# The Hadamard turn of W2 without its trip through DRAM, weight units in more staging places, and the weight sums' transfers interleaved by group

## The chip, the cores and the metric

The program runs on one core of a Trainium2 chip. The metric is the device time of one execution in microseconds. The core has five engines with an instruction queue each: PE (TensorE: matmuls, with PEld for its weight loads), DVE (VectorE), ACT (ScalarE), POOL (GpSimd) and SP (SyncE, which here only issues transfers). SP's transfers stand in the hardware queue of the DMA engines, POOL's in the software queue.

## The reference

The input x is 16 sequences of 256 tokens and 512 channels, in float32.

```python
def fwht(x):                       # along the last axis (2048), times 1/sqrt(2048)
    ...
def _L0_ffn_ref(x, W1, W2, W3):
    up_gate = jnp.einsum('bsd,hd->bsh', x, W1)
    up_lin = jnp.einsum('bsd,hd->bsh', x, W3)
    hidden = jax.nn.silu(up_gate) * up_lin
    hidden = fwht(hidden)
    out = jnp.einsum('bsh,dh->bsd', hidden, W2)
    return out
x = x + jnp.tanh(g_xattn[0]) * _L0_xattn_ref(16, 256, 512, L0_xattn_time_decay, L0_xattn_time_first, _layernorm(x, axis=-1), ctx_2048)
x = x + jnp.tanh(g_ffn[0]) * _L0_ffn_ref(_layernorm(x, axis=-1), L0_ffn_W1, L0_ffn_W2, L0_ffn_W3)
```

`_L0_xattn_ref` is a scan over the 256 tokens of a sequence with an exponential decay for each channel (numerator and denominator). The hidden width is 2048. The transform of `hidden` is moved into W2: the kernel transforms W2 once and never the hidden values.

## The kernel before

The 4096 tokens go in 8 chunks of 512 tokens, two sequences each. A `Run` is what is done for one chunk; the first chunk is split into `Run(0)` and `Run(1)` (sequence a and b), and the others are runs 2 to 8. Every engine has its own list of instructions, written out by hand, with semaphore waits between the lists.

**Weights in three-pass form.** Every float32 weight is split into a float16 part and a bfloat16 rest (`hi` and `lo`), and each product is three matmuls. W1 and W3 come in 16 units of 128x1024 (`units`, 0.5 MB each; two units make a piece of W1 and W3 of 256 hidden channels). SP's `load_unit(n)` brings a unit to one of six staging places (`raw`), ACT's `unit_hi(n)` writes the float16 part to `wts`, DVE's `unit_lo(n)` clamps it and writes the rest, and `raw_lo` counts that. `put_plain(p)` then stores piece p in `up_stage` in DRAM.

**W2.** Its four quarters (`load_rows(q)`, 1 MB each) lie in the upper half of `wts`. PE's `mix_rows(i)` multiplies one of 16 tiles with the 128x128 Hadamard matrix `had`, ACT's `keep_rows(i)` copies it to `mixed`, SP's `put_rows(q)` stores a quarter in DRAM and `turn_rows(q)` reads it back turned. PE's `mix_slots(i)` multiplies with `across` (the 16x16 part of the transform), ACT's `tile_hi`, POOL's `tile_clamp`, PE's `less_hi` and ACT's `tile_lo` split the tile into the two parts of `w2`.

**The first chunk.** PE's `ahead(a, j)` does hidden tiles 0 to 3 of sequence a; `ffn(b)` then does, in 16 slots j, the gate and the linear product of tile j (both sequences from j = 4) and the down product of tile j - 2. On DVE each slot has `hidden_tile` and `hidden_lo`, and between them the scan and norm of run 2 (`FIRST_AT` says in which slot), units (`unit_slot`) and weight sums (`SUMS_AT`). DVE works through this list in order: what waits in it holds all behind it.

**The weight sums.** Runs 2 to 8 use a scheme with 7 products of blocks in place of 8, for which sums of blocks of W1 and W3 are needed. POOL makes them in DRAM, for four groups of four units: `copy_group(g)` copies, `add_first(g)` adds 1 MB, `add_rest(g)` adds twice 0.5 MB, each behind the landing of the one before. SP's `load_again(n)` loads the summed unit n (to one of three places `traw`), DVE's `weight_parts(n)` splits it, and SP's `put_sums(n)` stores it to `up_stage` from one of two places `tout`, which must have been stored before it is written again.

**Runs 2 to 8.** `pairs` walks over 8 pairs of hidden tiles; SP's `load_pair` brings 2 MB of `up_stage` for each to a ring of two places. `load_pair(Run(2), 0)` and `(Run(2), 1)` are the first two, and `put_factors` and `spread_factors` send the layer norm's factors through DRAM.

## Time and profile before

| | |
|---|---|
| median of 3 runs | 1058.53 us (1057.27 to 1059.4) |
| the profiled execution | 1057.33 us, span 1055.5 us |
| PE busy | 1000.7 us (95%) |
| DVE busy | 801.5 us (76%) |
| first pair of run 2 begins on PE | 214.71 us |
| DMA | 218.40 MB, mean 207 GB/s |

The span is from the first to the last instruction, and times in the trace are counted from its start. A busy share is an average over stages with different limits: the first 215 us are the first chunk and all preparation of weights, and the rest is runs 2 to 8. The share of a DMA queue is the time of its packets as a share of the time of 16 DMA engines.

### The profile page before, as it was taken

How to read it: one execution, taken by the hardware profiler on the slowest of the kernel's cores; microseconds unless marked ns; L12 is line 12 of the kernel's file. 1: busy time of each engine (PE TensorE's matmuls, PEld its weight loads, DVE VectorE, ACT ScalarE, POOL GpSimd, SP SyncE). 2: the span in 40 equal slices, each digit the busy share in tenths (PEclk: the TensorE clock that was granted, in tenths of full speed). 3: DMA queues.
4: the chain of work that ended last, by engine and by line, in shares of the span. 5: the costliest groups of instructions: out<-in, count | busy, mean ns of one | idle time of the engine just before them, and what ended most of it. 6: DMA issues, size and time to landing. Idle time of an engine off the chain costs nothing.

```text
span 1055.5 us, 17259 instructions
## 1 busy us (share of the span) xinstructions
PE 1000.7 (95%) x6826; PEld 685.7 (65%) x6892; DVE 801.5 (76%) x1304; ACT 440.8 (42%) x736; POOL 252.4 (24%) x196
## 2 busy tenths in 40 slices
PE   5789689989999999999999999999999999999998
PEld 2355334456677777767776777767777677767775
DVE  7966598899989994889668994899669994753333
ACT  6756351346243542444243542445243532522221
POOL 0142121111432124221322124222322124111111
PEclk9898899999999999999999999999999999999999
DMA  9999999995885446454645446454645433444331
GB/s 355 347 396 266 312 255 292 245 322 192 302 289 182 153 167 240 114 221 148 257 161 180 155 165 240 115 222 147 256 160 180 173 116 151 161 170 157 125 149 41
DMA packets 49729, 218.40 MB, mean 207 GB/s; under 512 B 9456, under 2 KB 26992, under 8 KB 38512
## 3 DMA queue, kind: packets, MB, share of 16 engines
q1 hardware_dynamic: 40816, 200.52, 52.8%
q0 software_dynamic: 8832, 16.78, 7.7%
q8 instruction: 54, 0.88, 0.3%
q14 instruction: 27, 0.22, 0.1%
HBM read 187.90 MB, written 46.16 MB: 222 GB/s over the span
## 4 chain that ended last, share of the span: by engine, by line
PE 66%; DVE 13%; DMA 11%; issue 5%; ACT 3%; SPq 1%; POOL 0%; another core or an unknown queue 0%; DVEq 0%; ACTq 0%
PE pl L730 8%; PE pl L732 8%; PE pl L731 8%; PE po L742 7%; PE po L744 7%; PE pg L730 6%; PE pg L732 6%; PE pg L731 6%; PE po L753 4%; PE po L751 3%; DMA up_sums<-w_t 2%; DVE work L1600 2%; DMA factor_rows<-tiny 2%; DVE x L1427 2%; DMA up_stage<-wts 2%
## 5 line engine op out<-in xcount | busy, mean ns | idle before, releaser
L1745 POOL TENSOR_TENSOR work<-work 128x512 bf16<-128x512 f32 x112 | 163.7, 1462 | 594.5 <-DVE work L1600 594.5
L742 PE MATMUL po<-work,w 128*128 128x512 f16 x456 | 173.0, 379 | 2.1 <-DVE x L1427 1.2
L744 PE MATMUL po<-work,w 128*128 128x512 f16 x456 | 172.8, 379 | 0.0
L1062 ACT ACTIVATE work<-work 128x256 f32<-128x256 f32 x168 | 68.4, 415 | 210.4 <-DVE work L1507 210.3
L730 PE MATMUL pg<-wts 128*128 128x256 f16 x448 | 122.5, 273 | 3.9 <-DVE work L1507 3.8
L1507 DVE TENSOR_TENSOR work<-pl,wts 128x256 f32<-128x256 f32 x168 | 65.1, 414 | 80.3 <-PE pl L732 77.7
L730 PE MATMUL pl<-wts 128*128 128x256 f16 x448 | 122.1, 273 | 0.6 <-ACT wts L1036 0.6
L731 PE MATMUL pg<-wts 128*128 128x256 bf16 x448 | 122.4, 273 | 0.0
L732 PE MATMUL pg<-wts 128*128 128x256 f16 x448 | 122.4, 273 | 0.0
L730 PE MATMUL pl<-xn,wts 128*128 128x256 f16 x448 | 122.3, 273 | 0.0
L731 PE MATMUL pl<-xn,wts 128*128 128x256 bf16 x448 | 122.3, 273 | 0.0
L732 PE MATMUL pl<-xn,wts 128*128 128x256 f16 x448 | 122.2, 273 | 0.0
L732 PE MATMUL pl<-wts 128*128 128x256 f16 x448 | 122.1, 273 | 0.0
L731 PE MATMUL pl<-wts 128*128 128x256 bf16 x448 | 122.1, 273 | 0.0
L1600 DVE TENSOR_SCALAR work<-work 128x512 f16<-128x512 f32 x112 | 90.4, 808 | 7.9
L753 PE MATMUL po<-work,w 128*128 128x512 bf16 x228 | 86.4, 379 | 2.9
L1036 ACT COPY wts<-pg 128x512 f32<-128x512 f32 x56 | 32.6, 582 | 122.8 <-PE pg L732 122.8
L742 PEld LDWEIGHTS po<-work,w 128*128 128x128 f16 x456 | 44.6, 98 | 52.3 <-DVE x L1427 9.3
L744 PEld LDWEIGHTS po<-work,w 128*128 128x128 bf16 x456 | 44.6, 98 | 39.6
L730 PE MATMUL pg<-xn,wts 128*128 128x256 f16 x224 | 61.3, 274 | 6.3 <-DVE work L1383 3.6
L1507 DVE TENSOR_TENSOR work<-pg,early 128x256 f32<-128x256 f32 x56 | 23.6, 421 | 55.7 <-PE pg L732 54.8
L751 PE MATMUL po<-work,w 128*128 128x512 bf16 x172 | 65.2, 379 | 0.0
(201 smaller groups left out, 2132.8 us busy)
## 6 DMA issues: line engine op xcount, KB each, us to landing
wts<-up_stage SPq DMA_DIRECT2D x56, 2048.0 KB, 7.9
up_stage<-wts SPq DMA_DIRECT2D x8, 1024.0 KB, 11.8
up_stage<-wts SPq DMA_DIRECT2D x16, 512.0 KB, 8.4
ev<-ctx_t SPq DMA_DIRECT2D x7, 1024.0 KB, 11.3
xin<-x_t SPq DMA_DIRECT2D x7, 1024.0 KB, 8.2
bv<-x_tok SPq DMA_DIRECT2D x7, 1024.0 KB, 10.5
out_t<-x SPq DMA_DIRECT2D x7, 1024.0 KB, 4.8
wts<-up_sums SPq DMA_DIRECT2D x11, 512.0 KB, 11.4
```

The source lines that it names most:

```text
L730: pe.matmul(bank, hi, ah, start=(start and k == 0), stop=False, skip_group_check=True)
L731: pe.matmul(bank, hi, al, start=False, stop=False, skip_group_check=True)
L732: mm = pe.matmul(bank, lo, ah, start=False, stop=(stop and k == 1), skip_group_check=True)
L742: pe.matmul(po[:, d, :], w2h[:, j, d * P:d * P + P], hh[:, b, :], start=start, stop=False, skip_group_check=True)
L744: pe.matmul(po[:, d, :], w2l[:, j, d * P:d * P + P], hh[:, b, :], start=False, stop=False, skip_group_check=True)
L751: pe.matmul(po[:, d, :], w2h[:, j + 1, d * P:d * P + P], hl[:, b + 1, :], start=False, stop=False, skip_group_check=True)
L753: pe.matmul(po[:, d, :], w2h[:, j, d * P:d * P + P], hl[:, b, :], start=False, stop=((p - 1) % PAIRS == PAIRS - 1), skip_group_check=True) ...
L1036: act.copy(early1[:, w, :], chain_fifth[w]).then_inc(kept1, 1)
L1062: act.activation(sg[:, slot, cols], src, ACT.Silu, scale=(1.0, -1.0)[slot]).then_inc(acted, 1)
L1507: dve.tensor_tensor((sg, hf)[w][:, slot, b * T:b * T + T], bank, other, ALU.add).then_inc(joined, 1)
L1600: dve.tensor_scalar(hh[:, 2 * (p % 2) + slot, :], hf[:, slot, :], F16_MAX, -F16_MAX, ALU.min, ALU.max).then_inc(pair_hi, 1)
L1745: pool.tensor_tensor(hl[:, b, :], hf[:, slot, :], hh[:, b, :], ALU.subtract).then_inc(pair_lo, 1)
```

## The change

**W2.** The order of the two multiplications is swapped: W2 comes in another order of rows and columns, `mix_slots(i)` is now four float32 matmuls with the weight block as stationary operand and `across` as moving operand (128 columns each), which also turns the block; ACT's `keep(i)` copies the bank, with its columns permuted, to `mixed`, and `mix_rows(i)` multiplies with `had` from there. `put_rows`, `turn_rows` and the DRAM buffer `turn` are gone. **Units.** `raw` has 14 places, eight of them in the rows of W2 that have been used (`places`), so units 2 to 15 have waits on `slots_mm` and `rows_mm`. **Slots.** Units 14 and 15 are split in slot 12 of `ffn(b)`, and weight sum 3 moves from slot 8 to slot 5. **Sums.** POOL issues `copy_group(0)` behind the third clamp, and its `ffn` sends the first adds of group g + 1 and the copy of group g + 2 ahead of the third add of group g. **Orders.** The lists of SP, PE, ACT and DVE are written out anew, so that `over(a)` and `residual(a, 0)` stand ahead of the scans of sequence b.

```diff
 BETWEEN = {0: (), 1: (), 2: (10,), 3: (11,), 4: (13,), 5: (15,)}
@@ -71,7 +70,7 @@
...
-        raw = [psum2[:, :, :].rearrange("p k n -> p (k n)"), wide[:, 0:2, :].rearrange("p k n -> p (k n)"),
-               half1[:, 0:unit], half1[:, unit:], xn1[:, 0:unit], xn1[:, unit:]]
+        raw = ([psum2[:, :, :].rearrange("p k n -> p (k n)"), wide[:, 0:2, :].rearrange("p k n -> p (k n)")]
+               + [r[:, h * unit:(h + 1) * unit] for r in rows for h in range(2)]
+               + [r[:, h * unit:(h + 1) * unit] for r in (half1, xn1) for h in range(2)])
...
+        unit_slot = {0: (8, 9), 1: (10, 11), 3: (12,), 4: (13,), 12: (14, 15)}
+        places = (0, 1, 2, 3, 4, 5, 0, 1, 6, 7, 8, 9, 10, 11, 12, 13)
+
+        def uses(n):
+
+            return places[:n + 1].count(places[n])
...
+                if uses(n) > 1:
+                    sp.wait_ge(raw_lo, n - 5)
+                elif 2 <= places[n] < 10:
+                    sp.wait_ge(slots_mm, KT * (places[n] // 2))
+                elif places[n] >= 10:
+                    sp.wait_ge(rows_mm, KT * (places[n] // 2 - 2))
                 w, p = units[n]
-                sp.dma_start(raw[place_of[n]], raw_in[w][p]).then_inc(raw_loaded[place_of[n]], 16)
+                sp.dma_start(raw[places[n]], raw_in[w][p]).then_inc(raw_loaded[places[n]], 16)
 
             def load_rows(q):
                 sp.dma_start(rows[q], w2_in[q]).then_inc(rows_loaded[q], 16)
-
-            def put_rows(q):
-                sp.wait_ge(kept, KT * q + KT)
-                sp.dma_start(turn[q], mixed[q].rearrange("p (j d) -> p j d", d=P)).then_inc(put[q], 16)
-
-            def turn_rows(q):
-                sp.wait_ge(put[q], 16)
-                sp.dma_start(rows[q].rearrange("p (s d) -> p s d", d=P),
-                             turn[q].rearrange("(s r) j d -> (r j) s d", r=PS)).then_inc(turned[q], 16)
...
-            put_rows(0)
             load_half_x(1)
-            put_rows(1)
-            turn_rows(0)
-            put_rows(2)
-            turn_rows(1)
-            put_rows(3)
-            turn_rows(2)
-            for n in range(2, 4):
-                load_unit(n)
-            turn_rows(3)
-            for n in range(4, 6):
-                load_unit(n)
-            load_v(1)
-            for n in range(6, 10):
+            for n in range(2, 8):
                 load_unit(n)
             put_plain(0)
+            load_v(1)
+            load_unit(8)
+            load_unit(9)
             put_plain(1)
+            load_unit(10)
+            load_unit(11)
             load_x(1)
+            load_unit(12)
+            load_unit(13)
             sp.wait_ge(xn_turned, 4)
             load_tokens(1)
-            load_unit(10)
-            load_unit(11)
             put_plain(2)
-            load_unit(12)
-            load_unit(13)
+            load_unit(14)
+            load_unit(15)
+            put_plain(3)
             for n in range(0, 3):
                 load_again(n)
-            put_plain(3)
-            load_unit(14)
-            load_unit(15)
             put_plain(4)
...
             put_sums(1)
             put_plain(6)
+            load_again(4)
             put_sums(2)
-            put_plain(7)
+            load_again(5)
+            put_sums(3)
+            load_again(6)
             load_v(2)
-            load_again(4)
-            load_again(5)
+            put_sums(4)
+            load_again(7)
             load_x(2)
             load_tokens(2)
-            put_sums(3)
-            load_again(6)
-            put_sums(4)
-            load_again(7)
             put_sums(5)
+            put_plain(7)
+            put_factors(Run(3))
             load_pair(Run(2), 0)
-            put_factors(Run(3))
             put_sums(6)
             spread_factors(Run(3))
...
+            def mix_slots(i):
+
+                pe.wait_ge(rows_loaded[i // KT], 16)
+                wait(pe, kept, i)
+                for g in range(BLOCKS):
+                    col = (i % KT * BLOCKS + g) * P
+                    mm = pe.matmul(po[:, 2, g * P:(g + 1) * P], rows[i // KT][:, col:col + P], across,
+                                   start=True, stop=True)
+                mm.then_inc(slots_mm, 1)
+
             def mix_rows(i):
-                pe.wait_ge(rows_loaded[i // KT], 16)
-                wait(pe, kept, i - KT + 1)
-                pe.matmul(po[:, i % KT, :], had, tile_rows(i), start=True, stop=True).then_inc(had_mm, 1)
-
-            def mix_slots(i):
-                pe.wait_ge(turned[i // KT], 16)
-                if i < W2_BANKS:
-                    pe.wait_ge(kept, TILES)
-                wait(pe, w2_lo, i - W2_BANKS + 1)
-                pe.matmul(po[:, i % W2_BANKS, :], across, tile_rows(i), start=True, stop=False,
-                          skip_group_check=True).then_inc(blk_mm, 1)
+
+                pe.wait_ge(kept, i // KT * KT + KT)
+                wait(pe, w2_lo, i - 2)
+                pe.matmul(tile_banks[i % 3], had, mixed[i // KT][:, (i % KT) * TOK:(i % KT + 1) * TOK],
+                          start=True, stop=False, skip_group_check=True).then_inc(rows_mm, 1)
...
             scan(a, v, bv, scan_a)
             with_token(a, v, bv, scan_a, num_done)
             weigh(b)
+            over(a)
+            residual(a, 0)
             scan(b, ea, eb, scan_b)
-            over(a)
+            unit_lo(0)
+            x1_moments_of(0)
+            scan(b, v, bv, scan_a)
+            with_token(b, v, bv, scan_a, num_done)
+            unit_lo(1)
             with_token(b, ea, eb, scan_b, den_done)
-            residual(a, 0)
-            scan(b, v, bv, scan_a)
-            x1_moments_of(0)
-            for n in range(0, 2):
+            turned_lo(0)
+            for n in range(2, 4):
                 unit_lo(n)
-            turned_lo(0)
-            with_token(b, v, bv, scan_a, num_done)
             over(b)
             residual(b, 1)
-            dve.wait_ge(put[0], 16)
-            dve.wait_ge(put[1], 16)
-            hidden_tile(a, 0)
-            for n in range(2, 4):
-                unit_lo(n)
+            dve.wait_ge(rows_mm, 2 * KT)
+            for j in range(0, 2):
+                hidden_tile(a, j)
+            unit_lo(4)
             x1_moments_of(1)
-            for j in range(1, 3):
+            unit_lo(5)
+            for j in range(2, 4):
                 hidden_tile(a, j)
             turned_lo(1)
-            hidden_tile(a, 3)
-            unit_lo(4)
+            for n in range(6, 8):
+                unit_lo(n)
...
-                    tile_clamp(i)
-                add_rest(0)
-                for g in range(1, len(GROUPS)):
-                    copy_group(g)
-                    add_first(g)
-                    add_rest(g)
+                for g in range(len(GROUPS)):
+                    add_second(g)
+                    if g + 1 < len(GROUPS):
+                        add_first(g + 1)
+                    if g + 2 < len(GROUPS):
+                        copy_group(g + 2)
+                    add_third(g)
...
-            hidden_lo(Run(0), 0)
-            for i in range(6, 8):
+            copy_group(0)
+            for i in range(3, 11):
                 tile_clamp(i)
-            hidden_lo(Run(0), 1)
-            copy_group(0)
-            for i in range(8, 11):
+            pool.wait_ge(rows_mm, 2 * KT)
+            for j in range(0, 2):
+                hidden_lo(Run(0), j)
+            add_first(0)
+            copy_group(1)
+            for i in range(11, 13):
                 tile_clamp(i)
             for j in range(2, 4):
                 hidden_lo(Run(0), j)
-            add_first(0)
+            for i in range(13, TILES):
+                tile_clamp(i)
             ffn()
```

The list of POOL, which issues all transfers of the weight sums. Before, from the first clamps of W2 (L1682) on; L1677 is the low part of a hidden tile, L1694 a copy of a group, L1705 the first adds, L1714 the second and L1717 the third:

```order
L1682 TENSOR_SCALAR w<-w 128x4x128 x2
L1677 TENSOR_TENSOR work<-work 128x256
L1694 DMA up_sums<-w_t 16x16384 x2
L1682 TENSOR_SCALAR w<-w 128x4x128 x3
L1677 TENSOR_TENSOR work<-work 128x256 x2
L1705 DMA up_sums<-w_t 512x1x256 x2
L1682 TENSOR_SCALAR w<-w 128x4x128 x5
L1714 DMA up_sums<-up_sums 256x256 x2
L1717 DMA up_sums<-up_sums 256x256 x2
L1694 DMA up_sums<-w_t 16x16384 x2
L1705 DMA up_sums<-w_t 512x1x256 x2
```

And now, from the first copy on (L1695 clamps, L1690 low parts, L1707 copies, L1718, L1727 and L1734 first, second and third adds):

```order
L1707 DMA up_sums<-w_t 16x16384 x2
L1695 TENSOR_SCALAR w<-w 128x4x128 x8
L1690 TENSOR_TENSOR work<-work 128x256 x2
L1718 DMA up_sums<-w_t 512x1x256 x2
L1707 DMA up_sums<-w_t 16x16384 x2
L1695 TENSOR_SCALAR w<-w 128x4x128 x2
L1690 TENSOR_TENSOR work<-work 128x256 x2
L1695 TENSOR_SCALAR w<-w 128x4x128 x3
L1727 DMA up_sums<-up_sums 256x256 x2
L1718 DMA up_sums<-w_t 512x1x256 x2
L1707 DMA up_sums<-w_t 16x16384 x2
L1734 DMA up_sums<-up_sums 256x256 x2
```

The third adds of group 0, on which the first `load_again` waits, have moved behind the copy of group 1, the first adds of group 1 and the copy of group 2.

The list of SP at the same place. Before, from the tokens of run 2 (L409) on; L377 loads units, L418 is `put_plain`, L429 `load_again`, L435 `put_sums`:

```order
L409 DMA bv<-x_tok 128x2x1024
L377 DMA xn<-w_t 128x1024 x2
L418 DMA up_stage<-wts 128x4096
L377 DMA psum<-w_t 128x1024
L377 DMA wide<-w_t 128x1024
L429 DMA wts<-up_sums 128x1024 x2
L429 DMA spare<-up_sums 128x1024
L418 DMA up_stage<-wts 128x4096
L377 DMA xn<-w_t 128x1024 x2
L418 DMA up_stage<-wts 128x4096 x2
L435 DMA up_stage<-wts 128x2048
L429 DMA wts<-up_sums 128x1024
```

And now, from units 8 and 9 on (L379 loads units, L399 x, L402 the tokens, L411 is `put_plain`, L422 `load_again`, L428 `put_sums`):

```order
L379 DMA wts<-w_t 128x1024 x2
L411 DMA up_stage<-wts 128x4096
L379 DMA wts<-w_t 128x1024 x2
L399 DMA xin<-x_t 128x2048
L379 DMA x<-w_t 128x1024 x2
L402 DMA bv<-x_tok 128x2x1024
L411 DMA up_stage<-wts 128x4096
L379 DMA xn<-w_t 128x1024 x2
L411 DMA up_stage<-wts 128x4096
L422 DMA wts<-up_sums 128x1024 x2
L422 DMA spare<-up_sums 128x1024
L411 DMA up_stage<-wts 128x4096 x2
```

All units and `put_plain(3)` now stand ahead of the first `load_again`; before, two units and `put_plain(3)` stood behind it, ahead of the first `put_sums`.

## Rows read from the trace of the kernel before

**Rows 1.** The page: DMA busy tenths in 40 slices; shares of the last chain.

```profile
DMA  9999999995885446454645446454645433444331
...
PE 66%; DVE 13%; DMA 11%; issue 5%; ACT 3%; SPq 1%; POOL 0%; another core or an unknown queue 0%; DVEq 0%; ACTq 0%
```

**Rows 2.** Stages by window: PE, PEld, DVE, ACT, POOL busy, clock, DMA share, GB/s.

```profile
0.00:59.00 59.00, 40.08 (x132) 20.65 (x133) 48.51 (x99) 39.93 (x64) 7.76 (x15) 0.88 0.99 354
...
112.00:133.00 21.00, 12.88 (x51) 5.75 (x50) 15.18 (x21) 6.63 (x7) 1.03 (x2) 0.76 1.09 342
...
150.00:215.00 65.00, 58.53 (x257) 26.07 (x260) 55.07 (x81) 22.39 (x25) 13.11 (x13) 0.97 0.98 236
```

**Rows 3.** The chain that ended last, 60 to 150: start, us, what.

```profile
65.37 9.23 DMA up_sums<-w_t
...
74.90 15.42 DMA up_sums<-w_t
...
90.61 4.12 DMA up_sums<-up_sums
...
95.01 4.74 DMA up_sums<-up_sums
...
99.83 11.37 DMA wts<-up_sums
...
113.20 17.14 DMA up_stage<-wts
```

**Rows 4.** Timeline of PE: start, us, what, in brackets the idle time before and its releaser.

```profile
124.43 1.09 PE L589 MATMUL pst<-mats,bv 128*128 128x128 f32 x4 [8.07 <-ACT ev L881]
...
214.71 0.37 PE L730 MATMUL pg<-xn,wts 128*128 128x256 f16 x1 [3.64 <-DVE work L1383]
...
232.30 0.28 PE L730 MATMUL pg<-xn,wts 128*128 128x256 f16 x1 [1.36 <-DMA wts<-up_stage]
```

**Rows 5.** Timeline of DVE, the same columns.

```profile
111.22 0.69 DVE L1446 TENSOR_SCALAR wts<-wts 128x1024 f16<-128x1024 f32 x1 [5.30 <-DMA wts<-up_sums]
...
115.02 0.42 DVE L1433 TENSOR_SCALAR wts<-wts 128x1024 f16<-128x1024 f16 x1
...
116.62 0.42 DVE L1433 TENSOR_SCALAR wts<-wts 128x1024 f16<-128x1024 f16 x1
...
130.44 0.69 DVE L1446 TENSOR_SCALAR wts<-spare 128x1024 f16<-128x1024 f32 x1 [5.16 <-DMA up_stage<-wts]
...
176.59 2.35 DVE L1322 TENSOR_TENSOR eb<-x,pst 128x1024 f32<-128x1024 f32 x2 [3.76 <-PE pst L620]
...
200.83 0.69 DVE L1446 TENSOR_SCALAR wts<-wts 128x1024 f16<-128x1024 f32 x1 [2.86 <-DMA up_stage<-wts]
```

**Rows 6.** DMA queues: whole span, 0 to 59, 98 to 133, 104 to 107.

```profile
q0 software_dynamic: 8832, 16.78, 7.7%
...
q1 hardware_dynamic: 7903, 20.86, 98.7%
...
q1 hardware_dynamic: 1597, 7.48, 57.4%
q0 software_dynamic: 1642, 3.65, 45.8%
...
q0 software_dynamic: 32, 1.05, 93.3%
```

**Rows 7.** Timelines of ACT and POOL around the first hidden tiles.

```profile
53.43 0.38 ACT L961 ACTIVATE work<-pg 128x256 f32<-128x256 f32 x1
...
56.53 0.39 ACT L961 ACTIVATE work<-pg 128x256 f32<-128x256 f32 x1 [1.26 <-PE pg L656]
...
54.84 0.71 POOL L1677 TENSOR_TENSOR work<-work 128x256 bf16<-128x256 f32 x1 [1.36 <-DVE work L1390]
```

**Rows 8.** Timeline of PE: float32 matmuls of W2 and float32 transposes of x1.

```profile
13.12 4.46 PE L630 MATMUL po<-wts,mats 128*128 128x512 f32 x10
...
33.69 0.66 PE L603 MATMUL pst<-mats,x 128*128 128x128 f32 x4 [1.32 <-DVE x L1305]
34.19 0.60 PE L603 MATMUL pg<-mats,x 128*128 128x128 f32 x4
```

More of the change, by code:

```diff
@@ L707, in ffn @@
                     if j == 0:
-                        for i in range(11, 14):
-                            mix_slots(i)
-                        less_hi(11)
-                    if j == 1:
-                        less_hi(12)
-                        mix_slots(14)
-                        mix_slots(15)
                         for i in range(13, TILES):
@@ L1121, in _ @@
+            tile_hi(0)
             unit_hi(0)
-            for i in range(9, 16):
-                keep_rows(i)
-            unit_hi(1)
+            keep(5)
+            tile_lo(0)
+            for i in range(1, 3):
+                tile_hi(i)
+            keep(6)
+            unit_hi(1)
+            tile_lo(1)
+            unit_hi(2)
+            keep(7)
+            unit_hi(3)
+            tile_lo(2)
+            keep(8)
+            for i in range(3, 5):
+                tile_hi(i)
+            keep(9)
@@ L1125, in _ @@
+            tile_lo(3)
+            x1_normalise(0)
+            keep(10)
+            for i in range(5, 7):
+                tile_hi(i)
+            turned_hi(0)
+            tile_lo(4)
+            keep(11)
+            for i in range(5, 7):
+                tile_lo(i)
+            tile_hi(7)
             logs(b)
+            keep(12)
             inverses(b)
-            for i in range(0, 2):
-                tile_hi(i)
-            x1_normalise(0)
-            tile_hi(2)
-            for i in range(0, 2):
-                tile_lo(i)
@@ L1133, in _ @@
[L1133 to L1149 removed]
+            tile_lo(7)
@@ L1150, in _ @@
+            keep(13)
+            act.wait_ge(rows_mm, KT)
+            silu(a, 0)
             for i in range(8, 11):
                 tile_hi(i)
-            turned_hi(1)
+            silu(a, 1)
             unit_hi(4)
-            silu(a, 3)
+            keep(14)
+            unit_hi(5)
+            keep(15)
             for i in range(8, 11):
                 tile_lo(i)
+            x1_normalise(1)
+            silu(a, 2)
+            for i in range(11, 13):
+                tile_hi(i)
+            silu(a, 3)
@@ L1157, in _ @@
+            tile_lo(11)
+            turned_hi(1)
+            tile_lo(12)
+            for i in range(13, 16):
+                tile_hi(i)
+            for n in range(6, 8):
+                unit_hi(n)
             ffn(b)
@@ L1714, in add_rest, with add_third @@
                     pool.dma_start(sums[w][:, 3 * half:], sums[w][:, 0:half], accum_op=ALU.add).then_inc(summed[g][w], 16)
+            def add_third(g):
+                sums, half = group(g)[1], unit // 4
                 for w in range(2):
@@ L1807 @@
         had = np.block([[had, had], [had, -had]])
-    across = np.kron(np.eye(PS, dtype=np.float32), had[0:SLOTS, 0:SLOTS]) / np.float32(32)
+    across = np.kron(had[0:SLOTS, 0:SLOTS], np.eye(PS, dtype=np.float32)) / np.float32(32)
     gates = np.broadcast_to(np.concatenate([np.asarray(g_xattn), np.asarray(g_ffn)]), (P, 2))
```

174 lines of the change are left out of this document (77 added, 97 removed).

## The prediction

> **What bounds the kernel now.** I read the page first. The last chain is two thirds PE, and the DMA engines are at nine tenths for the first ninth of the span and at four to six tenths behind it [rows 1]. The change touches nothing behind the first pairs of run 2, so I looked at the time until that run's first pair begins on PE, 214.71 us [rows 4]. By stages [rows 2] PE has 12.88 of 21 us in 112 to 133 and 58.53 of 65 us in 150 to 215, DVE 15.18 and 55.07, while the DMA share stays at about 1.0 from the start to 215. So neither engine is full, and the DMA engines are.
>
> The waits say who is late. PE's longest is 8.07 us, ended at 124.43; before the first pair it waits 3.64 us for DVE's hidden tile 15, and before the second 1.36 us for the ring's load [rows 4]. DVE waits 5.30 us for the first loaded weight sum (until 111.22), 5.16 us for a place of `tout` to be stored (130.44), 3.76 us for the channel mean, on PE, and 2.86 us for `tout` again [rows 5]. The chain shows where the first comes from: copy of group 0 at 65.37, first adds at 74.90, second at 90.61, third at 95.01, `load_again(0)` from 99.83 to its landing 11.37 us later, and then `put_sums(0)`, 17.14 us [rows 3]. Behind slot 3 of `ffn(b)` DVE's list therefore runs from the landing of the first sum (call it T, 111.22) to PE's first pair at 214.71: 103.5 us, of which 5.16 + 3.76 + 2.86 = 11.8 us are waits. So what decides is when T falls, and what waits are left behind it.
>
> **The change part by part.**
>
> *The turn removed.* 4 MB are no longer written and 4 MB no longer read, 8.4 MB of the hardware queue. In 0 to 59 that queue moved 20.86 MB in 98.7% of 59 us, 2.8 us per MB [rows 6]: 23.4 us of the DMA engines are freed before 59. That is worth time only if something waits for the engines there; the next step asks that.
>
> *PE's work for W2.* Sixteen products with `across` become 64 of 128 columns with a weight load each. The trace has no such float32 matmul. Before, five of 512 columns (x10 in the row: two passes each) take 4.46 us [rows 8], 0.86 us with overlap taken off; a transpose with its own float32 load has a pitch of (34.19 - 33.69)/4 = 0.125 us [rows 8], so four matmuls of two passes lie between 0.86 us (by columns, loads hidden) and 1.0 us (eight such pitches). At half clock both double. I take 0.9, equal to what it replaces: nothing, 2 us over all 16 at most, hidden behind DVE's scans. The Trainium skill (TensorE: Matmul & The Clock Gate, Weight-path perf modes) says that fast weight loads are not to be had for float32. By the row they are hidden all the same; if they were not, each load being as long as its matmul, 14 us of PE work would be added ahead of slot 0.
>
> *ACT's, DVE's and POOL's lists until the first adds.* `add_first(0)` now stands behind the low parts of hidden tiles 0 and 1 of sequence a. Before, `silu` of these ended at 53.8 and 56.9, and a low part ended 2.1 us behind its `silu`'s start [rows 7]. ACT's list up to the first of them loses two copies of W2 and gains seven splits of about 0.5 us, 2.5 us, and loses waits for `load_unit` and `less_hi` that were about as long; DVE's has one product of 1.7 us more ahead of the first up tile, which then begins near 47. I take the two `silu` at 53.5 and 55.8, the low part at 58, and the first adds, which take a moment to issue, as work from 59.6 on (74.90 before [rows 3]).
>
> *The queue of POOL from there.* The sums cost 7.7% of 1055.5 = 81.3 us of all 16 engines for four groups, 20.3 each. A copy of 1.05 MB takes 93.3% of 3 us = 2.8 [rows 6], so a group's two take 5.6 and its adds 14.7 us: first 7.35, second 3.7, third 3.7. Ahead of the third add of the group's first half stand now: first adds of groups 0 and 1 (14.7), copies of 1 and 2 (11.2), second adds of 0 (3.7), and half a third (1.85): 31.4 us. Before it was half of that, with the copy. In the same time SP sends units 10 to 15, x, tokens, and `put_plain` 2 and 3: 7 MB, 7.34 in the row's unit, at 57.4% of 35 us for 7.48 MB, 2.7 us per MB [rows 6], 19.8 us. Both queues share the engines: in 98 to 133 the sum is 103% [rows 6]. (31.4 + 19.8)/1.03 = 49.7, so the sum is complete at 59.6 + 49.7 = 109.3. Then the load: 11.37 us before, when two copies were in the way [rows 3], and at least the 4.12 us of the shortest transfer of sums there; now small packets of adds are in the way, and I take 5.7. **T = 115.0**, against 111.22. The freed 23.4 us lie ahead of 59, where the queues now run dry, and the interleaving spends the 15 us by which the first adds start earlier.
>
> This T doesn't hang on DVE: before, it was ready at 111.22 - 5.30 = 105.9 [rows 5], and units 2 to 11 come sooner now, so it is ready between 97 and 106.
>
> *Behind T.* One unit fewer is split there (three for four): 116.62 - 115.02 = 1.6 us [rows 5]. `put_sums(0)` finds two `put_plain` ahead of it where three and two units stood, so its wait falls from 5.16 to about 4; sum 3 is now in slot 5 too and must wait for `put_sums(1)`, 2.5 (from 0 to 6: a store of 0.5 MB at full rate up to the 17.14 us of row 3); the mean's 3.76 goes, since DVE arrives later than PE there; the 2.86 goes, since sums 6 and 7 now stand in two slots, but ACT's root is then waited for, 0.8. Waits: 11.8 becomes 7.3. T to first pair: 103.5 - 1.6 - 4.5 = 97.4, and the pair begins at 212.4, 2.3 us earlier.
>
> *Ring and factors.* `put_factors` now stands ahead of the 2 MB load. Its wait for the factors held SP, and with that pair 1's load, so that PE waited 1.36 us [rows 4]; this goes. `put_plain(7)` now stands ahead of the first ring load and waits for unit 15, split in slot 12 some 18 us before the pair; the load of 2 MB needs 5.7 us of the engines, which are by then rid of the sums.
>
> The sum: 2.3 + 1.4 = 3.7 us. From the profiled execution's 1057.33 us that is 1053.6, and its time is 1.2 us under the median of the runs. From the median it is 1054.8. **I predict 1054 us.**
>
> **The rivals.** About 0.2%, 2.1 us, is what a measurement of this kernel can tell from no change.
>
> *The first sum is in time.* If the adds were as cheap per byte as loads, or overlapped with them, T would be set by DVE. With T between 97 and 106 and 94 to 97 us behind it, the pair begins at 191 to 203: 13 to 25 us faster, 1033 to 1046. For it speaks that DVE and PE are both short of full [rows 2]; against it the adds' 1 KB packets, 81 us for 16.78 MB [rows 6]. The Trainium skill's fit (DMA: Bandwidth & Descriptors, Anatomy of one DMA) gives the moving part of a transfer as its bytes at 436 GB/s, which for the 31.4 us would be about 15 and T would be DVE's. The trace disagrees: 81.3 us against 38.
>
> *Slower.* One mechanism: copies of later groups stand in the engines when SP's loads and stores of sums come, as at 99.83, where a load took 11.37 and the store 17.14 us [rows 3]. The load then costs 5.7 more, and the waits for both places of `tout` about 5.6 more: 3.7 faster becomes 7.6 slower, 1062 to 1066. It decides from T = 118.7 on, 3.7 us past mine.
>
> *No difference.* The part ahead of T gives exactly what it takes and only the ring's 1.4 us are left; or the turn wasn't on any path. 1057 to 1060.
>
> **How the numbers follow.** Chances: my forecast (1048 to 1056) 0.40, first sum in time 0.18, no difference 0.20, slower 0.22. Of the forecast's cases some 0.03 lie within 2.1 us of before. So faster 0.55, same 0.23, slower 0.22. The forecast's own range is 1048 to 1056; for 8 in 10 I go down into the first rival's middle, 1040, and up to 1064.
>
> **What would show it.** Right: first adds near 58 (POOL), the DMA share under a half between 37 and 58, the third add of group 0 landing at 107 to 113, DVE idle 10 us or more ahead of its first weight sum at about 115, then short waits for stores in slot 5, and the first pair at 212 with PE waiting for DVE's hidden tile 15. Wrong: a first sum before 105, which makes it much faster; ACT so late in the first 60 us that the first adds start past 65; or a wait of DVE for `tout` over 8 us in slot 5.

## The result, and the profile after

The changed kernel takes 1068.1 us (median of 6 runs, 1067.02 to 1068.79), the kernel before 1058.46 us beside it (6 runs, 1056.18 to 1059.4). The ratio is 1.0093, 95% interval 1.0075 to 1.0112: slower, where the prediction said 1054 us, and above the range's end of 1064.

The profiled execution has a span of 1066.9 us, 11.4 more than before. The page of the changed kernel, its DMA slices and the shares of its last chain, which answer to [rows 1]:

```profile
DMA  9599998586585546355554456254745434444331
...
PE 68%; DVE 16%; DMA 8%; issue 5%; ACT 3%; DVEq 0%; SPq 0%; POOL 0%; ACTq 0%
```

The page only tells that the engines of the DMA are now less full in the second slice (26.7 to 53.3). The place is told by the windows (columns as in [rows 2]; the last line is the kernel before):

```profile
0.00:59.00 59.00, 40.85 (x230) 30.60 (x230) 50.05 (x102) 43.20 (x70) 13.48 (x22) 1.00 0.80 297
...
37.00:58.00 21.00, 16.44 (x105) 11.22 (x104) 20.20 (x37) 17.31 (x28) 4.30 (x6) 1.00 0.75 279
...
133.00:150.00 17.00, 5.80 (x27) 2.45 (x25) 9.41 (x9) 0.00 (x0) 4.06 (x4) 0.78 1.04 271
...
133.00:150.00 17.00, 16.95 (x79) 7.74 (x79) 15.79 (x13) 7.52 (x10) 3.51 (x5) 1.00 1.08 325
```

The DMA share until 59 fell from 0.99 to 0.80: the freed time is there. But in 133 to 150 PE works 5.80 of 17 us (16.95 before) and ACT not at all, while the DMA engines are full. The chain of the changed kernel, which answers to [rows 3], says what they carry:

```profile
76.17 14.14 DMA up_sums<-up_sums
...
90.60 20.51 DMA up_sums<-up_sums
111.20 8.90 DMA wts<-up_sums
120.13 0.70 DVE wts L1457
125.52 0.70 DVE wts L1457
127.50 14.85 DMA up_stage<-wts
142.44 0.70 DVE wts L1457
```

The second adds of group 0 go out at 76.17 (90.61 before), but the third adds, issued at 90.60, take 20.51 us where they took 4.74. The first load starts at 111.20 and T, DVE's first work on a loaded sum, is 120.13, against 111.22. Then a place of `tout` waits 14.85 us for its store. The timelines of DVE, PE and ACT of the changed kernel, in the columns of [rows 4, 5]:

```profile
120.13 0.69 DVE L1457 TENSOR_SCALAR wts<-wts 128x1024 f16<-128x1024 f32 x1 [22.21 <-DMA wts<-up_sums]
138.28 0.69 DVE L1457 TENSOR_SCALAR wts<-spare 128x1024 f16<-128x1024 f32 x1 [8.88 <-DMA up_stage<-wts]
142.44 0.69 DVE L1457 TENSOR_SCALAR wts<-wts 128x1024 f16<-128x1024 f32 x1 [2.20 <-DMA up_stage<-wts]
187.03 2.35 DVE L1333 TENSOR_TENSOR eb<-x,pst 128x1024 f32<-128x1024 f32 x2 [2.52 <-PE pst L603]
223.57 0.68 DVE L1394 TENSOR_TENSOR work<-work,pl 128x512 f32<-128x512 f32 x1
...
154.51 0.59 PE L641 MATMUL pg<-xn,wts 128*128 128x512 f16 x1 [15.71 <-ACT work L960]
226.06 0.39 PE L710 MATMUL pg<-xn,wts 128*128 128x256 f16 x1 [3.80 <-DMA wts<-up_stage]
...
151.32 2.56 ACT L895 ACTIVATE ev<-ev,cc 128x512 f32<-128x512 f32 x4 [26.67 <-DVE eb L1263]
```

PE's 15.71 us are put down to ACT, but ACT stood still until 151.32: it waited for DVE's scan of run 2 (L1263), and the scan stands in DVE's list behind the two waits for `tout`. The first pair of run 2 begins at 226.06, 11.35 us later than before, and behind it both kernels need 840.8 us (1055.5 - 214.71 and 1066.9 - 226.06). So the loss lies ahead of the first pair: 8.9 us until T, 1.7 us of the ring's load (PE starts 1.81 us behind the end of DVE's hidden tile 15 at 224.25, and 0.15 us before), and 0.8 us between.

### The profile page after: what moved, and what is told of

Same layout as the page of the kernel before. It is cut to its first block, busy times and chain, and to the rows that moved or that the text cites. A ratio compares the mean times of both kernels' runs of the same rounds, so it can differ in the third digit from the quotient of the medians.

```text
span 1066.9 us, 17504 instructions
## 1 busy us (share of the span) xinstructions
PE 1003.7 (94%) x6988; PEld 694.6 (65%) x6988; DVE 802.4 (75%) x1304; ACT 440.0 (41%) x736; POOL 254.1 (24%) x196
## 4 chain that ended last, share of the span: by engine, by line
PE 68%; DVE 16%; DMA 8%; issue 5%; ACT 3%; DVEq 0%; SPq 0%; POOL 0%; ACTq 0%
PE pl L712 8%; PE pl L710 8%; PE pl L711 8%; PE po L722 7%; PE po L724 7%; PE pg L710 6%; PE pg L712 6%; PE pg L711 6%; PE po L733 4%; PE po L731 4%; DMA up_sums<-up_sums 3%; DVE x L1438 2%; DMA wts<-up_stage 2%; DVE work L1611 2%; DMA up_stage<-wts 1%
## 5 line engine op out<-in xcount | busy, mean ns | idle before, releaser
L731 PE MATMUL po<-work,w 128*128 128x512 bf16 x228 | 86.4, 379 | 0.0
L733 PE MATMUL po<-work,w 128*128 128x512 bf16 x228 | 86.4, 379 | 0.0
L724 PEld LDWEIGHTS po<-work,w 128*128 128x128 bf16 x456 | 44.6, 98 | 39.3
```

The source lines that it names most:

```text
L724: pe.matmul(po[:, d, :], w2l[:, j, d * P:d * P + P], hh[:, b, :], start=False, stop=False, skip_group_check=True)
L731: pe.matmul(po[:, d, :], w2h[:, j + 1, d * P:d * P + P], hl[:, b + 1, :], start=False, stop=False, skip_group_check=True)
L733: pe.matmul(po[:, d, :], w2h[:, j, d * P:d * P + P], hl[:, b, :], start=False, stop=((p - 1) % PAIRS == PAIRS - 1), skip_group_check=True) ...
```

## The experiments

"In the old order" means that POOL issues the sums group by group, as before the change. Each row's time stands beside its own runs of the kernel before. T and the first pair are read in the profiled execution.

| kernel | us | ratio to before, interval | T | first pair |
|---|---|---|---|---|
| before | 1058.46 | | 111.22 | 214.71 |
| changed | 1068.1 | 1.0093 (1.0075 to 1.0112) | 120.13 | 226.06 |
| e1: old order | 1047.21 | 0.9904 (0.9869 to 0.9939) | 104.20 | 205.10 |
| e2: factors behind the load | 1065.42 | 1.0074 (1.0049 to 1.0098) | 120.49 | 224.20 |
| e3: sum 3 in slot 8 | 1062.97 | 1.0051 (1.0035 to 1.0068) | 119.74 | 220.04 |
| e4: before, interleaved | 1072.8 | 1.0142 (1.0111 to 1.0173) | 127.22 | 232.02 |
| e5: e1 + e2 + e3 | 1044.49 | 0.9879 (0.9857 to 0.99) | 103.57 | 199.91 |
| e6: only first adds held | 1056.73 | 0.9998 (0.9981 to 1.0014) | 109.85 | 215.88 |
| e7: group 0 clear | 1056.8 | 0.9992 (0.9973 to 1.0011) | 104.10 | 216.18 |
| e8: old order, first adds late | 1054.18 | 0.997 (0.9951 to 0.9988) | 109.95 | 211.78 |
| e9: e1 + e2 | 1050.25 | 0.9904 (0.988 to 0.9928) | 102.65 | 201.33 |
| e10: e5, copy held | 1052.26 | 0.9921 (0.9901 to 0.9942) | 96.37 | 197.95 |
| e11: e1 + e3 | 1044.66 | 0.9847 (0.9822 to 0.9871) | 103.74 | 204.22 |
| e12: e11, copy held | 1050.93 | 0.9906 (0.988 to 0.9932) | 96.78 | 206.65 |

### The order of the sums, alone

**e1** undoes the interleaving and keeps all else:

```diff
-                for g in range(len(GROUPS)):
-                    add_second(g)
-                    if g + 1 < len(GROUPS):
-                        add_first(g + 1)
-                    if g + 2 < len(GROUPS):
-                        copy_group(g + 2)
-                    add_third(g)
+                add_second(0)
+                add_third(0)
+                for g in range(1, len(GROUPS)):
+                    copy_group(g)
+                    add_first(g)
+                    add_second(g)
+                    add_third(g)
...
             add_first(0)
-            copy_group(1)
```

> Edit: the changed kernel with POOL's order of before for the sums (second and third adds of group 0 directly behind its first adds, then copy, first, second, third of groups 1 to 3, no copy of group 1 ahead). Theory A (the interleaving makes the first sum late): the software queue then holds 12.9 us of work ahead of the third add in place of 31.4, so it lands near 90 in place of 111, DVE finds the first sum at 98 to 100 in place of 120.1, and the first pair of run 2 begins at 197 to 203 in place of 226: 1038 to 1046 us. Rival B (SP's own transfers and the 1 KB packets of the adds make it late, whatever their order): third add still past 105, 1062 to 1068. Rival C (DVE or PE would bound that stage anyway): the first sum is early but the first pair begins no earlier than 215.

**e4** does the reverse: the kernel before, with `add_rest` parted in two and POOL's new order.

> Edit: the kernel before with the new order of the sums in POOL alone (copy of group 1 directly behind the first adds of group 0; first adds of the next group and copy of the one after it ahead of the third adds). Theory A: 18.5 us more of the DMA engines' work stands ahead of the first sum, which DVE finds at 125 to 130 in place of 111.2, and with the same 103.5 us behind it the kernel takes 1072 to 1077. Rival B (order in POOL's queue is irrelevant): 1057 to 1060.

e1 is 0.96% faster than before and so some 2% faster than the changed kernel; e4 is 1.4% slower than before. Both signs agree: the interleaving costs, in the changed kernel as in the one before, and the rest of the change, taken together, is a gain. e4 came out as expected (T 125 to 130, 1072 to 1077 us). e1's mechanism is that of its theory A, but its numbers lie just past the expected ones (T 98 to 100, first pair 197 to 203, 1038 to 1046 us): the third adds landed at 92.8 and not near 90, and the load took 11.30 us. POOL's issues and the chain of e1:

```profile
60.75 2.74 POOL L1718 DMA_DIRECT2D up_sums<-w_t  x2
...
92.28 1.35 POOL L1707 DMA_DIRECT2D up_sums<-w_t  x2
...
86.95 5.83 DMA up_sums<-up_sums
92.87 11.30 DMA wts<-up_sums
104.20 1.01 DVE wts L1457
```

The first adds go out at 60.75, as in the changed kernel (60.33), but the third adds take 5.83 us and the sum is ready 18.3 us sooner (92.87 against 111.20). Behind the first pair e1 needs 839.9 us, within 1 us of the 840.8 of the other two.

### What an interleaved transfer costs

**e6** holds only the next group's first adds behind the third adds, and keeps the copies interleaved:

```diff
                 for g in range(len(GROUPS)):
                     add_second(g)
-                    if g + 1 < len(GROUPS):
-                        add_first(g + 1)
                     if g + 2 < len(GROUPS):
                         copy_group(g + 2)
                     add_third(g)
+                    if g + 1 < len(GROUPS):
+                        add_first(g + 1)
```

> The changed kernel, but the first adds of group g + 1 stand behind the third add of group g; the copies stay interleaved (group 1 behind the first adds of group 0, group g + 2 behind the second adds of g). Theory: what stands ahead of the third adds costs its own work of the DMA engines, one for one. In the old order the sum of group 0 lands at about 92.9; two copies are 11.2 us of all engines, so here it lands at about 104 and T is 112 to 116, against 104.2 in the old order and 120.1 with all interleaved; the time lies between the two, 1054 to 1062 us. Rival: copies in large packets cost the sums in flight next to nothing and only the small packets of the next first adds do; then T is 104 to 107 and the time 1047 to 1051.

**e7** sums group 0 alone and interleaves from group 1 on:

```diff
+                add_second(0)
+                add_third(0)
+                copy_group(1)
+                add_first(1)
+                copy_group(2)
-                for g in range(len(GROUPS)):
+                for g in range(1, len(GROUPS)):
                     add_second(g)
...
             add_first(0)
-            copy_group(1)
```

> The changed kernel with group 0 summed alone (nothing between its adds), and the interleaved order from group 1 on. If all of the interleaving's cost is the lateness of the first sum: T at 104 to 106 and 1047 to 1050 us. If the interleaving also costs behind T, because copies and first adds of groups 2 and 3 stand in the engines when SP stores sums 0 and 1: the same T, but DVE's waits for tout are 8 to 11 us in place of 4.8, and the time is 1051 to 1056.

Here are the times from a group's first issue to the load that waits for its third adds. For group 0 it runs from POOL's first adds to `load_again(0)`, for group 1 from POOL's copy to `load_again(4)`. "Work put between" is by the prediction's prices (a copy of a group 5.6 us of all engines, its first adds 7.35).

| pair of kernels | group | interleaved | not | difference | work put between |
|---|---|---|---|---|---|
| changed, e1 | 0 | 111.20 - 60.33 = 50.9 | 92.87 - 60.75 = 32.1 | 18.8 | 18.55 |
| e4, before | 0 | 120.33 - 76.07 = 44.3 | 99.83 - 74.90 = 24.9 | 19.3 | 18.55 |
| e6, e1 | 0 | 102.87 - 59.52 = 43.4 | 32.1 | 11.2 | 11.2 |
| e7, e1 | 1 | 149.72 - 92.53 = 57.2 | 131.11 - 92.28 = 38.8 | 18.4 | 18.55 |

What is issued ahead of a group's third adds delays them by its own work, one for one within 5%, in four comparisons of one trace each. e6's rival (large packets of the copies cost nothing) falls. The rows behind the two new ones: e6's issues of POOL and its chain,

```profile
59.52 2.75 POOL L1718 DMA_DIRECT2D up_sums<-w_t  x2
...
89.56 13.22 DMA up_sums<-up_sums
102.87 6.96 DMA wts<-up_sums
```

and in e7 POOL's copy of group 1, SP's `load_again(4)` with the `put_sums(2)` behind it, the KB of these two and their us from issue to landing, and DVE on T and on sum 4:

```profile
92.53 1.35 POOL L1707 DMA_DIRECT2D up_sums<-w_t  x2
...
149.72 0.32 SPq L422 DMA_DIRECT2D wts<-up_sums  x1
150.08 0.43 SPq L428 DMA_DIRECT2D up_stage<-wts  x1
...
wts<-up_sums SPq DMA_DIRECT2D x1, 512.0 KB, 8.7
up_stage<-wts SPq DMA_DIRECT2D x1, 512.0 KB, 10.5
...
104.10 0.77 DVE L1457 TENSOR_SCALAR wts<-wts 128x1024 f16<-128x1024 f32 x1 [5.72 <-DMA wts<-up_sums]
160.64 0.69 DVE L1457 TENSOR_SCALAR wts<-wts 128x1024 f16<-128x1024 f32 x1 [15.22 <-DMA up_stage<-wts]
```

e7 gave what neither of its two theories said in full. T is that of e1, and yet the pair comes 11 us later. The cost has moved from group 0 to group 1. DVE stands 15.22 us ahead of sum 4 in slot 8, until 160.64. The profile puts that down to a place of `tout`, whose store landed at 160.6 (150.08 + 10.5): SP's list has `load_again(4)` ahead of `put_sums(2)`, so the late sum of group 1 also holds a store of group 0's sum. But sum 4 itself landed only at 158.4 (149.72 + 8.7). So 13.0 of the 15.22 us are the late sum, and at most 2.2 are SP's order. I had expected 8 to 11 us of waits for `tout` in all; the profile has 20.1. The time, 1056.8, lies just past the 1051 to 1056 expected. In e1 the same load goes out at 131.11, and DVE doesn't wait in slot 8.

e6's time is within its expectation (1054 to 1062); its T is 109.85 where 112 to 116 were expected, since the load took 6.96 us and not 9 to 11.

### When the first adds start

**e8** is e1 with `add_first(0)` behind the low parts of tiles 2 and 3, as before the change.

```diff
-            add_first(0)
             for i in range(11, 13):
                 tile_clamp(i)
             for j in range(2, 4):
                 hidden_lo(Run(0), j)
+            add_first(0)
```

> The changed kernel with the old order of the sums, and the first adds of group 0 behind the low parts of hidden tiles 2 and 3, as before the change: issued at about 73 in place of 60.8 (74.9 before). If the gain of the old order over the kernel before (11 us) is the earlier start of the first adds: the sum lands at 97 to 101, T is 108 to 112 and the time is 1051 to 1057 us. If the start doesn't matter since the DMA engines free of W2's turn would let the adds finish anyway by the time DVE is ready (98.1): T at 104 to 106, 1047 to 1050.

The first adds go out at 72.60, 11.9 us later than in e1, the load at 99.97, 7.1 later, and the time is 7 us above e1's (0.997 against 0.9904 of before). T is 109.95, as the first of the two theories has it (108 to 112). So of e1's gain of 0.96% about two thirds is the earlier start of the first adds, and 0.3% is the rest of the change.

### The other two costs behind T

**e2** puts the factors behind the first ring load:

```diff
-            put_factors(Run(3))
             load_pair(Run(2), 0)
+            put_factors(Run(3))
```

> Edit: put_factors stands again behind the first ring load. Theory A (the 4-byte pieces of the factors hold the hardware queue in front of the 2 MB load): the load lands by 222, PE waits for DVE's hidden tile 15 alone and begins the first pair at 224.4 in place of 226.1, but SP waits for the factors again before the second ring load, which gives about 1 us back: 1066 to 1068. Rival (the load takes 19.6 us for its size or for put_plain(7) in front of it): the first pair stays at 226 and the time at 1068.

**e3** moves sum 3 back: `SUMS_AT = {..., 5: (2,), 8: (3, 4), ...}`.

> Edit: weight sum 3 back in slot 8. Theory A (its 8.9 us wait for a place of tout in slot 5 is new and on the path): DVE's wait at 142 goes and the first pair begins 5 to 9 us earlier, 1060 to 1064. Rival (DVE would wait for something else, or PE bounds the stage behind it): under 2 us, 1067 to 1069.

In e2 PE no longer waits for the ring's load but 2.14 us for DVE's hidden tile 15, and the first pair is 1.9 us earlier; the interval (1.0049 to 1.0098) overlaps the changed kernel's, so its time isn't told apart from it. e3 is told apart: 1.0051, 4.4 us faster by the ratios. From T to the first pair it needs 100.3 us where the changed kernel needs 105.9, for one of two waits for `tout` in slot 5 is gone (7.59 us remain of 11.1) and so is most of the mean's (0.7 us remain of 2.5).

In e2 and e3 the first pair is where theory A had it.

**e5** takes all three edits together, **e9** leaves out e3's, **e11** e2's.

> The old order of the sums on POOL, the factors behind the first pair's load, and sum 3 in slot 8, all three in the changed kernel. If the three costs lie at three places: the old order alone gave 1047.2 us; PE's wait for the ring's load ahead of the first pair was 4.33 us there, of which the factors' place should give 2 to 3.5; sum 3 gives less than the 5 us it gave in the changed kernel, since the two waits for tout came to 4.8 us in the old order and not to 11.1: 0 to 2.5. So 1042 to 1045 us, T at 104 to 105, the first pair at 200 to 203. If sum 3 is worth its whole 5 us apart from the order, 1039 to 1041. If the factors' place only moves the wait on to DVE's hidden tile 15, no less than 1046.

> The changed kernel with the old order of the sums and the factors behind the first pair's load, sum 3 left in slot 5. It shares out the 2.7 us by which all three edits (1044.5 us) beat the old order alone (1047.2 us). If they come from the ring's load: first pair at 202.5 to 203.5 with PE waiting about 2 us for DVE's hidden tile 15 and no longer 4.3 us for the load, and 1044 to 1046 us. If they come from sum 3's slot: the first pair's wait falls but the second pair's load comes later, and 1046.5 to 1048 us.

> The changed kernel with the old order of the sums and sum 3 in slot 8, the factors ahead of the first pair's load as in the changed kernel. The factors' place gave nothing in the old order (0.9904 of before with and without it), so the 2.6 us of all three edits should be sum 3's: ratio 0.986 to 0.989, first pair at 201 to 204 after a wait of about 4 us for the ring's load, no wait over 4 us for the factors behind it. If the three together are more than their parts, the ratio is 0.990 or above.

The factors' place is worth nothing in the old order: e9's ratio is e1's, 0.9904. Its first pair is 3.8 us earlier, and PE then waits 6.49 us in the pair for DVE, which waits for the factors that now land about 1 us later:

```profile
201.33 0.27 PE L710 MATMUL pg<-xn,wts 128*128 128x256 f16 x1 [2.13 <-DVE work L1394]
...
217.99 0.40 PE L710 MATMUL pg<-wts 128*128 128x256 f16 x1 [6.49 <-DVE work L1518]
...
DVE ev L1234 <- DMA wts<-factor_rows: 6.2, 1, 6.2
```

My expectation for e9 (1044 to 1046 from the ring's load) missed; that for e5 (1042 to 1045) held. e11 is a little better than expected (0.9847, where 0.986 to 0.989 stood), but in its trace PE waits 5.70 us for the ring's load, not about 4, and its first pair is only 0.9 us ahead of e1's; e1's interval and e11's touch (0.9869 and 0.9871). That sum 3's slot is worth something in the old order is therefore likely and not shown. e5 and e11 are the fastest that ran, 1.2% and 1.5% below before; which of them is the better is not settled.

### The copy behind the loads

In e1 and e5 the copy of group 1 is issued 0.6 us ahead of the first load, which then takes 11 us. **e10** is e5, **e12** is e11, with that copy held back until the loads have landed:

```diff
                 add_third(0)
+                for n in range(TRAWS):
+                    pool.wait_ge(traw_loaded[n], 16)
                 for g in range(1, len(GROUPS)):
                     copy_group(g)
```

> All three edits, and POOL issues the copy of group 1 only when loads 0 to 2 of the sums have landed. In the kernel with all three the copy was issued at 91.93, ahead of the load at 92.48, which took 11.06 us. Theory: the load is slow because of the copy's packets in the same engines; without them it takes 4 to 6.5 us, DVE is ready at 97.4, so T is 97.5 to 99 in place of 103.57. The sum of group 1 moves back by some 6 to 8 us, to 137 to 139 in place of 131, and its first load is wanted by DVE at about 136 to 141: so half to all of the gain is given back by a wait for sum 4; 1040 to 1045 us. Rival: a load of sums takes about 9 to 11 us whatever stands beside it, since the loads and stores that SP issues with it share the engines; then T stays at 102 or more and the time is 1045 to 1050.

> The same as the run beside it (old order, sum 3 in slot 8, factors ahead), and POOL issues the copy of group 1 only when loads 0 to 2 have landed. With the factors behind the load this gave the earliest first pair (197.95) but 9.2 us of waiting for the factors. If that wait comes of the factors' place: T at 96 to 98, first pair at 199 to 202 behind a wait of 3 to 5 us for the ring's load, the wait for the factors 2 to 5 us, ratio 0.981 to 0.986. If an earlier first pair always finds the factors late, since they hang on the scan and norm of run 2 and on engines that the last sums fill: the wait for them stays at 7 us or more and the ratio is 0.988 to 0.993.

DVE no longer waits for the first sum at all: T is 96.37 and 96.78, when DVE comes to it. The load took 4.5 us in both, where it took 11.1 in e5 and 10.5 in e11: it was slow because of the copy, as theory had it. But the gain is gone by the first pair or just behind it, and both kernels are slower than e5 and e11 (1052.26 us, where 1040 to 1045 stood, and 1050.93). In e10 DVE waits 9.2 us for the factors, in e12 7.7 us, and PE waits for the ring:

```profile
206.65 0.39 PE L710 MATMUL pg<-xn,wts 128*128 128x256 f16 x1 [9.80 <-DMA wts<-up_stage]
...
181.00 1.17 SPq L443 DMA_DIRECT2D wts<-up_stage  x1
```

The lead of 7 us at T had shrunk to 2.2 by sum 2 (114.36 against 116.58 in e11), because DVE now came early to other things: it waited 5.4 us for PE's products and again for `tout`. The ring's load was issued only 1.7 us earlier than in e11 (182.67), and landed 2.4 us later. Group 3's first adds had moved from 174.82 to 177.32, and the software queue carries more of the sums beside the load. The queues of e12 in 181 to 206 and of e11 in 182.7 to 204 (packets, MB, share of 16 engines):

```profile
q1 hardware_dynamic: 1532, 3.92, 74.9%
q0 software_dynamic: 1231, 1.21, 45.4%
...
q1 hardware_dynamic: 1541, 3.96, 78.5%
q0 software_dynamic: 703, 0.68, 37.4%
```

So 1.21 MB of adds lie beside the ring's load in e12, 0.68 in e11. But the place of the factors weighs more: in e10, with the same copy held back and the load ahead of the factors, the load took 13.8 us where it took 25.6 in e12 (the last section has all kernels). How much the adds alone cost the load isn't shown; no run took them away. My expectation for e12 (0.981 to 0.986) missed, and its rival's range (0.988 to 0.993, wait for the factors at 7 us or more) held.

## Why the prediction was wrong

**What it had right.** The first adds go out at 60.33 (58 to 59.6 predicted), the sum of group 0 is complete at 111.1 (90.60 + 20.51; predicted 109.3, within 107 to 113), and DVE is ready for it at 120.13 - 22.21 = 97.9 (97 to 106). From 60.3 to 111.1 the software queue took 64.4% of the engines, 32.7 us (31.4 predicted), and SP's transfers 39.3%, 20.0 us for 7.39 MB (19.8 for 7.34). PE's work for W2 costs about what was taken: the four matmuls of a tile end within 1.13 us, where 0.9 to 1.0 were predicted. `mix_rows` right behind them has as many columns and a quarter of the weight loads, and takes 1.02 us, so the weight loads are all but hidden:

```profile
28.35 1.13 PE L616 MATMUL po<-mats,wts 128*128 128x128 f32 x8 [0.36 <-ACT work L974]
29.32 1.02 PE L624 MATMUL po<-work,mats 128*128 128x512 f32 x2
```

The Trainium skill (TensorE: Matmul & The Clock Gate, Weight-path perf modes) has no fast weight loads for float32; by these rows the loads hide here all the same. The pricing of the sums by the row of their queue, 20.3 us a group, held to within 5% in four cases (the table above). The Trainium skill's fit (DMA: Bandwidth & Descriptors, Anatomy of one DMA), bytes at 436 GB/s, would make about 15 us of the 31.4 and put T near 99, an estimate by the prediction's own formula; this case's trace disagrees, T was 120.13.

**The steps that failed.** Predicted was a first pair at 212.4, measured 226.06: 13.7 us later. Four terms of the sum were mis-sized, by 13.9 us together; the other 0.2 were given back between them.

1. *T, 5.1 us.* The sum landed 1.9 us late, and the load, "I take 5.7", took 8.90. What stood beside it was what I had said, small packets of adds: in those 8.9 us the software queue moved 0.99 MB in 1009 packets. The price was wrong. I left out that POOL, its third adds once issued, goes on to the next group, so that the first adds of group 2 are in the engines and the copy of group 3 is issued when the sum of group 0 lands at 111.1 (POOL's issues; the software queue in 98 to 133, where [rows 6] had 45.8%):

```profile
106.96 1.31 POOL L1718 DMA_DIRECT2D up_sums<-w_t  x1 [2.18 <-DMA up_sums<-w_t]
109.70 1.29 POOL L1718 DMA_DIRECT2D up_sums<-w_t  x1 [1.42 <-DMA up_sums<-w_t]
110.32 1.70 POOL L1707 DMA_DIRECT2D up_sums<-w_t  x2
...
q0 software_dynamic: 2841, 6.29, 80.9%
```

2. *The waits for `tout`, 4.6 us.* Predicted 4 + 2.5, measured 8.88 + 2.20. The stores meet these transfers: `put_sums(1)` took 14.85 us. e3 and e1 confirm it from two sides: without sum 3 in slot 5 the waits are 7.6 us, and without the interleaved transfers 4.8.
3. *The mean, 2.5 us.* "Goes, since DVE arrives later than PE": DVE still waited 2.52 us for PE, and as long in e1, where the waits for `tout` are short. So it isn't the interleaving's; why it stays is open.
4. *The ring's load, 1.7 us.* "The load of 2 MB needs 5.7 us of the engines, which are by then rid of the sums". They were rid of them, but the load took 19.6 us (206.42 to 226.06), in part since it now stands behind the factors' transfer. In e2, where it stands ahead, it took 16.3, still far from 5.7, and PE waited for DVE alone; more of it in the last section.

To these come the 1.4 us of PE's wait ahead of the second pair. That wait is gone, but one of 0.97 us for DVE stands at 254.16, and behind the first pair both kernels need 840.8 us: nothing was gained there. With these 1.4 us the miss is 15.1, which is 1066.9 - 1051.8, the measured span and the predicted one.

**The reason behind the sizes.** Terms 1 and 2, 9.7 us, are one error. I priced the interleaved transfers once, in the landing of group 0's sum, and judged that they just spend the 15 us by which the first adds start earlier. They do that. But when the third adds land, the next groups' transfers already stand in the engines, and they are in the way of the loads, the stores, and the next sum. The rival "Slower" named this mechanism and its turning point, T = 118.7; T was 120.1. It priced itself at 7.6 us, and the measured loss is 9.6. That they lie so close is in part luck: it had 5.7 us more for the load where 3.2 came, 5.6 more for `tout` where 4.6 came, and neither the mean nor the ring's load; and beside the first load stood adds, not the copies that it names. Its chance of 0.22 was too low, since the row from which I took the load's price, 11.37 us with two copies in the way [rows 3], was nearer to this case than the bound of 4.12.

The question that the working never asked is what the kernel would do without the interleaving. e1 answers it: the order before gives T = 104.2, and all of the early start is kept. e8 shows that this start is worth about 7 us.

What I also didn't foresee is that the freed time of the engines in 37 to 58 would in part be used: the share there is 0.75, where I expected less than a half. It isn't on the path.

**What stays open.** Whether e11 or e5 is better, and whether a finer order of the groups than one behind the other (a copy of the next group between the stores of sums, say) gives more than 1.5%. Both attempts at T alone gave it back, e10 in the wait for the factors and e12 at the ring's load.

## What to carry to other kernels

Here, with the DMA engines full (a share of 1.04 in 75 to 92 of e1), a transfer issued ahead of another delayed it by its own work, one for one. By this, interleaving chains can help only where the engines would otherwise be idle between the links; no run here tried that case. Work out such a reordering not just for the first consumer but for each: who loads, who stores and which group is next, and, in smaller measure, what stands in the same list behind a wait for it (`put_sums(2)` behind `load_again(4)`, 2.2 us). And when a change mixes a gain with a reordering, price the change without the reordering too.

## What the runs showed of the hardware

**Adds in DRAM are dear by the MB.** In the 8.9 us of the first load of the changed kernel, 111.2 to 120.1 (packets, MB, share of 16 engines):

```profile
q0 software_dynamic: 1009, 0.99, 78.9%
q1 hardware_dynamic: 280, 1.05, 33.1%
```

The adds' packets of 1 KB take 0.789 x 8.9 / 0.99 = 7.1 us of all engines per MB, the loads beside them 2.8. The two shares add up to 112%, so both are somewhat too high.

**A pause behind a transfer of 4-byte elements.** The ring's load of 2 MB took 19.6 us with nothing in the software queue. The DMA slices of the changed kernel for 206.4 to 226.0 (one slice is 0.49 us), with `put_factors` issued at 205.82, its 1024 elements of 4 bytes being nearly all of the packets under 512 B:

```profile
DMA  9989759999000000000000099890179769897899
...
DMA packets 1465, 3.62 MB, mean 185 GB/s; under 512 B 1082, under 2 KB 1082, under 8 KB 1224
```

For some 6 us no engine shows work, though the load is outstanding. The same view of e3, 200 to 220, where the factors also stand ahead of the load, has the pause at the same distance, and that of e2, 205 to 226, where they stand behind it, has the engines busy from the load's start on, and the pause later:

```profile
DMA  2989894999000008000000099701597879979899
...
DMA  0299998899989999959999679989200000001767
```

So in these three traces the pause goes with the factors' transfer. In e2 it falls on the end of the load, which landed at 222.0, after 16.3 us. All kernels agree on the order (us from issue to landing of the first ring load):

| the load stands | |
|---|---|
| behind the factors | changed 19.6, e1 20.1, e3 19.3, e6 19.9, e7 18.6, e8 21.0, e11 21.5, e12 25.6 |
| ahead of them | before 13.7, e2 16.3, e4 8.2, e5 11.1, e9 12.0, e10 13.8 |

The rows of e11 and e5:

```profile
wts<-up_stage SPq DMA_DIRECT2D x1, 2048.0 KB, 21.5
...
wts<-up_stage SPq DMA_DIRECT2D x1, 2048.0 KB, 11.1
```

Four pairs of kernels differ in this order alone: changed and e2, e1 and e9, e11 and e5, e12 and e10. The load is 3.3, 8.1, 10.4 and 11.8 us shorter ahead of the factors. It buys little: e9 is as fast as e1, e5 no faster than e11, and in e9 and e10 DVE waits 6.2 and 9.2 us for the factors next. Why the factors' transfer holds the load isn't known from these runs: no kernel sent the factors in larger pieces, or from another queue, or left them out.
